# Two-layer adapted residual, fp32: tiles 0 and 1 multiplied in plain fp32, loads and selections reordered, last tile in two pieces

## What is computed

```python
x = x + einsum('bct,bcd->bdt', x, L0_weights[i0])      # (32,64,512), a 64x64 matrix for each sample
H = einsum('btd,od->bto', x, W)                        # 512x512, the same for all samples
xa = einsum('btd,brd->btr', x, A[i1])                  # rank 16, one of 8 adapters for each sample
x = x + H + einsum('btr,bor->bto', xa, Bm[i1]) * s[i1]
```

## Time and profile before

| | |
|---|---|
| median of 3 runs | 85.75 us (85.62 to 85.75) |
| profiled execution | 86.49 us |
| its span, first to last instruction | 84.5 us |
| TensorE, matmuls busy | 74.8 us, 89% |
| VectorE / ScalarE / GpSimd busy | 55.0 / 47.4 / 37.7 us |
| DMA | 14.58 MB, mean 173 GB/s |

### The profile page before, as it was taken

The page is one execution under the profiler, slowest core; times in us unless marked ns, Lnnn a source line. Parts: engine busy times, 40 slices in busy tenths (PEclk is TensorE's granted clock), DMA queues, the critical chain, the costliest instruction groups (busy, mean ns, idle before and its releaser), DMA issues.

```text
span 84.5 us, 1975 instructions
## 1 busy us (share of the span) xinstructions
PE 74.8 (89%) x498; PEld 70.0 (83%) x498; DVE 55.0 (65%) x132; ACT 47.4 (56%) x101; POOL 37.7 (45%) x83
## 2 busy tenths in 40 slices
PE   2985769938999999999999999999999999999650
PEld 2972569927999999999999999999999999999530
DVE  3898923696987567756865686568656865666230
ACT  0656200918777575757575757575767666463610
POOL 3075599974171656265526553645364541000000
PEclk9999999999999999999999999999999999999995
DMA  1896747999937848987796779868705550303033
GB/s 12 328 388 165 142 137 159 216 206 197 211 81 143 307 160 284 265 255 136 206 237 220 122 214 232 224 130 249 231 37 136 144 215 10 124 4 124 0 124 128
DMA packets 12797, 14.58 MB, mean 173 GB/s; under 512 B 6898, under 2 KB 7154, under 8 KB 12786
## 3 DMA queue, kind: packets, MB, share of 16 engines
q1 hardware_dynamic: 7458, 9.31, 37.5%
q0 software_dynamic: 4608, 4.22, 23.1%
q10 hardware_dynamic: 720, 0.92, 3.5%
HBM read 10.23 MB, written 4.19 MB: 171 GB/s over the span
## 4 chain that ended last, share of the span: by engine, by line
PE 76%; DVE 8%; DMA 6%; ACT 2%; ACTq 2%; issue 1%; POOL 1%; POOLq 0%; DVEq 0%
PE z_ps L489 54%; DMA scale_sb<-scales 6%; PE out_ps L523 5%; PE out_ps L527 4%; PE out_ps L530 4%; PE out_ps L524 4%; PE v_ps L514 4%; DVE moving L380 1%; DVE w_low L389 1%; POOL moving L221 1%; ACTq L262 1%; DVE a_scaled L437 1%; ACT b_high L291 1%; DVE b_stack L407 1%; DVE a_table L441 1%
## 5 line engine op out<-in xcount | busy, mean ns | idle before, releaser
L489 PE MATMUL z_ps<-moving,x_high 128*128 128x272 f32 x256 | 40.8, 299 | 2.6 <-POOL moving L221 1.4
L489 PEld LDWEIGHTS z_ps<-moving,x_high 128*128 128x128 f32 x256 | 36.7, 195 | 5.2 <-ACT moving L274 2.1
L398 DVE TENSOR_TENSOR z_low<-z_ps,z_high 128x240 fp32r<-128x240 f32 (+1 forms) x32 | 13.6, 424 | 17.3 <-ACT z_high L284 17.3
L228 POOL DMA_DIRECT2D b_raw<-b_t x32 | 19.7, 619 | 6.3 <-issue 6.2
L489 PE MATMUL z_ps<-moving,x_low 128*128 128x272 f32 x128 | 22.1, 297 | 0.0
L284 ACT ACTIVATE z_high<-z_ps 128x240 fp32r<-128x240 f32 (+1 forms) x32 | 12.3, 384 | 16.3 <-DVE low_rank L418 8.3
L489 PEld LDWEIGHTS z_ps<-moving,x_low 128*128 128x128 f32 x128 | 19.0, 197 | 0.0
L221 POOL CAST moving<-a_table 128x128 fp32r x32 | 9.0, 311 | 21.5 <-PE z_ps L489 20.6
L310 ACT ACTIVATE out_sb<-out_ps 128x512 f32<-128x512 f32 x15 | 9.0, 597 | 7.3 <-PE out_ps L530 7.3
L407 DVE TENSOR_TENSOR b_stack<-b_raw,b_high 128x512 fp32r<-128x512 f32 x16 | 11.1, 692 | 2.6 <-ACT b_high L291 2.6
L291 ACT ACTIVATE b_high<-b_raw,low_rows 128x512 fp32r<-128x512 f32 x16 | 11.4, 716 | 0.0
(11 more groups left out here) (33 smaller groups left out, 48.9 us busy)
## 6 DMA issues: line engine op xcount, KB each, us to landing
x_raw<-xt SPq DMA_DIRECT2D x16, 256.0 KB, 5.1
b_raw<-b_t POOLq DMA_DIRECT2D x32, 128.0 KB, 4.8
out<-out_sb SPq DMA_DIRECT2D x15, 256.0 KB, 4.0
w_raw<-w_t ACTq DMA_DIRECT2D x2, 256.0 KB, 3.2
w_raw<-w_t SPq DMA_DIRECT2D x2, 256.0 KB, 4.5
w_sb<-w SPq DMA_DIRECT2D x32, 16.0 KB, 3.7
a_raw<-a_t ACTq DMA_DIRECT2D x1, 256.0 KB, 5.1
out<-out_sb ACTq DMA_DIRECT2D x1, 128.0 KB, 1.7
```

The costliest lines, as they stand in the source:

```text
L228: pool.dma_start(b_raw[s * C:(s + 1) * C, t % BBUFS, :], b_t[ds(which[s], 1), :, :].to_broadcast([GROUPS, RANK, OUT]),).then_inc(b_loaded[ ...
L398: nc.vector.tensor_tensor(out=z_low[:, t % 2, col:col + n], in0=z, in1=z_high[:, t % 2, col:col + n].bitcast(fp32), op=ALU.subtract).then_ ...
L489: last = nc.tensor.matmul(z_ps[t % 2][:, bank, BANK_AT[bank]:BANK_AT[bank] + HALF], x[:, t % XBUFS, k * P:(k + 1) * P], moving[:, int(n == ...
```

## The change

- W is loaded in four pieces instead of four row blocks: first columns 0 to 271, then the rest, each in two halves of the rows (`PIECES`). x1 and A go ahead of the second column half, x2 ahead of w0. The scales move from ScalarE's queue to GpSimd's.
- The diagonal is added on VectorE in five parts (`DIAGONAL`), not on GpSimd.
- Tiles 0 and 1 (`PLAIN`) are multiplied in plain fp32 straight from `x_raw` and `w_raw`, four products for each bank instead of twelve. Their A columns are copied, scaled, into `w_raw` by ScalarE, which reads the indices itself. z is copied out whole (`z_plain`), and layer 0 is one fp32 matmul plus the low rank.
- TensorE's order: W bank of 0, A bank of 1, A bank of 0, W bank of 1; the low ranks and layer 0 of both lie among tile 2's banks.
- In the later tiles ScalarE and VectorE split B behind the low rank's v instead of ahead of z.
- The last tile's layer 0 is made in two pieces, A part and W part, in two PSUM tensors, with the layer 0 of tile 14 ahead of them and behind the last product.
- Eight warm-ups on a `warm` tile set by VectorE, not nine on the identity.

The diff, cut to its core:

```diff
+    PIECES = [(cols, rows) for cols in ((0, HALF), (HALF, OUT)) for rows in ((0, K // 2), (K // 2, K))]
+
+    DIAGONAL = ((0, 0, P, 0), (1, P, 2 * P, 0), (2, 2 * P, HALF, 1), (2, HALF, 3 * P, 3), (3, 3 * P, 4 * P, 3))
+
+    ADDED = (2, 3, 0, 5)
...
             load_x(0)
-            load_w(2)
+            load_w(1)
+            load_x(1)
             load_w(3)
+            load_x(2)
             sync.wait_ge(index_loaded, 16)
-            which = read_indices(sync, 0, 0, w0.shape[0], READ)
+            which = read_indices(sync, 0, 0, w0.shape[0], 2 * READ)
             sync.wait_ge(w0_cleared, 1)
             load_w0(which[0], 0)
-            load_x(1)
             load_w0(which[1], 1)
-            load_x(2)
-            which = read_indices(sync, 0, 2, w0.shape[0], READ)
-            load_w0(which[0], 2)
-            load_w0(which[1], 3)
             load_x(3)
+            load_w0(which[2], 2)
+            load_w0(which[3], 3)
             for t in range(4, TILES):
...
+            pool.dma_start(scale_sb[:], scales.rearrange("(a n) -> a n", a=1).to_broadcast([P, ADAPTERS]),
+                           ).then_inc(scales_loaded, 16)
             pool.wait_ge(ident_ready, 1)
             pool.wait_ge(index_loaded, 16)
-            which = read_indices(pool, 1, 0, ADAPTERS, READ)
-            for k in range(K):
-                add_diagonal(k)
+            which = read_indices(pool, 1, 0, ADAPTERS, 2 * READ)
+            pool.wait_ge(w_loaded[3], 16)
             load_b(which[0], 0)
             pool.wait_ge(a_ready, 1)
-            take_a(which[0], 0)
+            take_a(which[2], 2)
             load_b(which[1], 1)
             add_identity(0)
-            take_a(which[1], 1)
             add_identity(1)
-            for t in range(2, TILES):
+            load_b(which[2], 2)
+            take_a(which[3], 3)
+            add_identity(BATCH_OF[3])
+            load_b(which[3], 3)
+            for t in range(4, TILES):
...
             load_w(0)
-            load_w(1)
             act.dma_start(a_raw[:], a_t).then_inc(a_loaded, 16)
-            act.dma_start(scale_sb[:], scales.rearrange("(a n) -> a n", a=1).to_broadcast([P, ADAPTERS]),
-                          ).then_inc(scales_loaded, 16)
+            load_w(2)
             act.wait_ge(warm_ready, 1)
-            nc.scalar.activation(warm[0:1, 1:2], warm[0:1, 0:1], ACT.Copy)
-
-            def high_of_w(k):
-                act.wait_ge(w_diag, k + 1)
-                nc.scalar.activation(moving[:, 0, k, AC:AC + OUT], w_raw[:, k, :], ACT.Copy).then_inc(w_high_ready, 1)
+            nc.scalar.activation(warmed[:], warm[0:1, 0:1], ACT.Copy)
+            act.wait_ge(index_loaded, 16)
+            first = read_indices(act, 1, 0, ADAPTERS, PLAIN)
...
+            def take_raw_a(t):
+
+                at = 0 if t % 2 else AC + OUT
+                for s in range(PER):
+                    dst = w_raw[:, :, at + s * RANK:at + (s + 1) * RANK]
+                    src = a_raw[:, ds(first[t][s], 1), :].rearrange("p a (k r) -> p (a k) r", k=K)
+                    nc.scalar.activation(dst, src, ACT.Copy,
+                                         scale=scale_sb[:, ds(first[t][s], 1)]).then_inc(raw_cols_ready, 1)
...
+            def take_z(t, part):
+
+                z, col, n = z_part(t, part)
+                if part == A_PART:
+                    act.wait_ge(plain_rank_ready[t], 1)
+                else:
+                    act.wait_ge(w_bank_done, t + 1)
+                nc.scalar.activation(z_plain[:, t, col:col + n], z, ACT.Copy).then_inc(z_plain_ready[t], 1)
...
             high_of_w(0)
+            act.wait_ge(a_loaded, 16)
+            act.wait_ge(scales_loaded, 16)
+            take_raw_a(1)
+            take_raw_a(0)
             high_of_w(1)
+            take_z(0, W_PART)
+            act.wait_ge(a_scaled_ready, 1)
+            nc.scalar.activation(a_table[:, :, 0, :], a_scaled[:], ACT.Copy).then_inc(a_high_ready, 1)
             high_of_w(2)
             high_of_w(3)
-            act.wait_ge(a_scaled_ready, 1)
-            nc.scalar.activation(a_table[:, :, 0, :], a_scaled[:], ACT.Copy).then_inc(a_high_ready, 1)
+            take_z(1, A_PART)
+            high_of_x(2)
+            take_z(0, A_PART)
+            take_z(1, W_PART)
             act.wait_ge(low_rows_ready, 1 + PER)
-            high_of_z(0, A_PART)
             high_of_b(0)
-            high_of_z(0, W_PART)
             act.wait_ge(low_groups_ready, 1)
-            high_of_x(2)
             high_of_v(0)
-            high_of_z(1, A_PART)
             high_of_b(1)
+            high_of_v(1)
             high_of_x(3)
-            high_of_v(1)
+            high_of_z(2, A_PART)
+            high_of_x(4)
+            high_of_v(2)
+            high_of_b(2)
+            take_out(0)
+            take_out(1)
             last = TILES - 1
-            for t in range(2, TILES):
+            for t in range(3, last):
                 high_of_z(t - 1, W_PART)
-                high_of_b(t)
                 if t + 2 < TILES:
                     high_of_x(t + 2)
                 high_of_z(t, A_PART)
                 high_of_v(t)
-                if t == 2:
-                    take_out(0)
+                high_of_b(t)
                 take_out(t - 1)
+            high_of_z(last - 1, W_PART)
+            high_of_b(last)
+            high_of_z(last, A_PART)
+            high_of_v(last)
             high_of_z(last, W_PART)
+            take_out(last - 1)
+            _, col, n = z_part(last, A_PART)
             act.wait_ge(out_done, last + 1)
-            nc.scalar.activation(out_sb[:, last, 0:OUT // 2], out_ps[last % 2][:, 0:OUT // 2],
+            nc.scalar.activation(out_sb[:, last, col:col + n], out_ps[last % 2][:, 0:n],
                                  ACT.Copy).then_inc(out_ready, 1)
             act.wait_ge(out_ready, TILES)
-            act.dma_start(out[PER * last:, :, 0:OUT // 2].rearrange("s c l -> (s c) l"),
-                          out_sb[:, last, 0:OUT // 2]).then_inc(stored, 16)
+            act.dma_start(out[PER * last:, :, col:col + n].rearrange("s c l -> (s c) l"),
+                          out_sb[:, last, col:col + n]).then_inc(stored, 16)
             act.wait_ge(stored, 16 * (TILES + 1))
...
+            add_diagonal(0)
+            add_diagonal(1)
+            add_diagonal(2)
             dve.wait_ge(a_loaded, 16)
             dve.wait_ge(scales_loaded, 16)
             every = scale_sb[:].rearrange("p (a q) -> p a q", q=1).to_broadcast([P, ADAPTERS, K * RANK])
             nc.vector.tensor_tensor(out=a_scaled[:], in0=a_raw[:], in1=every, op=ALU.mult).then_inc(a_scaled_ready, 1)
-            low_of_w(2)
-            low_of_w(3)
+            low_of_w(0)
+            low_of_w(1)
+            add_diagonal(3)
+            add_diagonal(4)
             dve.wait_ge(a_high_ready, 1)
             nc.vector.tensor_tensor(out=a_table[:, :, 1, :], in0=a_scaled[:],
                                     in1=a_table[:, :, 0, :].bitcast(fp32),
                                     op=ALU.subtract).then_inc(a_ready, 1)
-            high_of_x(1)
-            low_of_x(1)
-            split_w0(0)
             dve.wait_ge(own_rank_ready, 1 + PER)
+            take_low_rank(1)
+            low_of_w(2)
+            low_of_w(3)
             take_low_rank(0)
-            low_of_z(0, A_PART)
+            low_of_x(2)
+            take_low_rank(2)
             low_of_b(0)
-            low_of_z(0, W_PART)
-            split_w0(1)
-            low_of_x(2)
             low_of_v(0)
-            take_low_rank(1)
-            low_of_z(1, A_PART)
             low_of_b(1)
+            low_of_v(1)
             low_of_x(3)
-            low_of_v(1)
+            low_of_z(2, A_PART)
+            low_of_x(4)
+            low_of_v(2)
+            low_of_b(2)
+            split_w0(BATCH_OF[2])
             last = TILES - 1
-            for t in range(2, TILES):
+            for t in range(3, last):
                 low_of_z(t - 1, W_PART)
-                low_of_b(t)
                 take_low_rank(t)
                 low_of_z(t, A_PART)
                 if t + 2 < TILES:
                     low_of_x(t + 2)
                 low_of_v(t)
+                low_of_b(t)
                 if t % 2 == 0:
                     split_w0(BATCH_OF[t])
+            low_of_z(last - 1, W_PART)
+            take_low_rank(last)
+            low_of_z(last, A_PART)
+            low_of_b(last)
+            low_of_v(last)
             low_of_z(last, W_PART)
-            dve.wait_ge(out_ready, TILES)
-            nc.vector.tensor_copy(out_sb[:, last, OUT // 2:], out_ps[last % 2][:, OUT // 2:]).then_inc(last_ready, 1)
+            _, col, n = z_part(last, W_PART)
+            dve.wait_ge(last_done, 1)
+            nc.vector.tensor_copy(out_sb[:, last, col:col + n], v_ps[(last + 1) % 2][:, 0:n]).then_inc(last_ready, 1)
...
+            def plain_products(t, part, ks):
+
+                at = FIRST[t % 2] + bank_of(t, part) * HALF
+                for k in ks:
```

(61 more changed lines are left out.)

162 lines of the change are left out of this document (92 added, 70 removed).

## The result

The changed kernel takes **83.02 us** (median of four executions) against 85.75 before: ratio 0.966, 95% interval 0.958 to 0.973. Now and then an execution of either kernel falls in a slower state (here one at 85.77, beside three at 82.84 to 83.03), and the ratios in this document leave such executions out. It is faster, by less than half of the 6.6 us forecast, and its time lies above the range of 77.8 to 82.3. Its profiled execution took 83.01 us.

The account below looks back on a forecast made before the run. It took TensorE (4.16 us a tile) to bound the even stretch and a relay of waits the beginning. Start 13.9 − 21.3, moved work +1.8, crossing +0.3, end −1.3 sum to −6.6: 85.75 to 79.1 us, range 77.8 to 82.3.

Parts of the forecast that it names:

- Price of a plain product: Tiles 0 and 1 on TensorE: a plain fp32 product of 272 columns takes 0.47 us fast, 0.945 slow.
- change of pace: Start: TensorE goes from slow to fast pace at 7.5 us, so tile 2 starts at 13.9.
- the pace changes late: Rival, start: TensorE's pace changes only at 11 us, losing 1.7 us, 80.8 us in all; chance 0.16.
- Do the data keep up?: Start: loads at 402 GB/s plus 0 to 1 us land before TensorE wants them, slack 1.2 or more each.
- The scales on GpSimd's queue: Start: the scales land at 3.9, 6.4 or 8.8 us, taken 6.4; ScalarE wants them at 5.6 to 7.
- helpers late: Rival: A copies or scales arrive 1.5 us late, or the crossing costs 1.5; 80.6 to 82.1 us, chance 0.16.
- The crossing: Behind tile 2's start, ScalarE and VectorE catch up on three tiles' work: +0.3 us, bounds 0 and 1.5.
- B behind the low rank costs nothing: Later tiles: splitting B behind the low rank costs nothing, as b_t is read only a tile later.
- The end: From last product to end: 4.5 us, 0.93 paid earlier before, against 4.9; −1.3 us, bounds −0.8 and −1.4.
- The period of 4.16: Even stretch of later tiles: TensorE's 4.16 us a tile stays unchanged.
- Slower: Rival: slow pace through all plain products, 85.5 us, or 86.7 with a slow first bank of tile 2; chance 0.04.
- no gain: Rival: a plain product costs twice the scaled pair, adding 6.6 us, 85.7 in all; chance 0.02.

Follow-up runs that it names:

- b0: The changed kernel itself run once more, with no edit, as a yardstick; ratio 0.957 to the kernel before.
- b2: Changed kernel without the scales' load (scale_sb set to 1) and with B of tile 1 loaded ahead of A's selection for tile 2; ratio 0.933.
- c3: Changed kernel with the scales' load doubled, the second into a buffer nothing reads; 83.89 us, one execution.
- e1: Kernel d1 with w0 of tiles 2 and 3 loaded ahead of x3 on SyncE's queue; ratio 0.925 to the kernel before.
- a3: Changed kernel with GpSimd's load of B for tile 1 moved ahead of A's selection for tile 2; ratio 0.940.
- c4: Changed kernel with B split ahead of the low rank again in tiles 3 to 14, as before the change; ratio 0.975.
- b3: Kernel before with the last-tile part of the change alone; ratio 0.987.
- d2: Kernel before with the scales loaded as one 32-byte row and spread by a matmul with ones; ratio 1.007.
- a1: Changed kernel with the scales' load back on ScalarE's queue, between W piece 0 and A; ratio 0.944.
- b1: Changed kernel with the edits of a1 and a3 together; ratio 0.949.
- d1: Changed kernel with scales as one row spread by matmul, and B of tiles 0, 1, 2 loaded in a row once W piece 1 landed; ratio 0.938.
- a4: Changed kernel with the load of x2 issued after w0 of tile 0; 83.08 us, one execution.

## Why the prediction was wrong

Predicted −6.65, measured −2.73: 3.9 us. Of this 0.5 is scale: the spans differ by 3.2, but the sum was made on an execution that was 0.74 above its median, and what lies around the span shrank by 0.28. The rest by the steps:

- **Price of a plain product and change of pace: held.** 0.45 against 0.47, and in after the pace changed at 7.3 against the 7.5 taken. Without its stand tile 2 would have started at 15.02 − 1.46 = 13.56, against 13.9. The 24 instructions behind 9.64 all run at the fast pace, and no slow pace past 8.5 was seen in after, so the rival *the pace changes late* falls. That 7.3 is so near 7.5 is luck: it was a choice without a row, and in b0, the same kernel, the pace had changed by 5.7.
- **"Do the data keep up?": the step that failed first, 1.3 us** (15.02 against 13.9; 0.16 of it from taking before's start from the chain and not the timeline). The sum gave x1 7.1 and piece 3 7.8, with 0 to 1 us on top; they came at 9.3 and 10.0, and the prediction's own sign of being wrong, a gap of TensorE between 5 and 14 us, is there. It counted bytes over 402 GB/s, and the scales are 4 KB. The runs put a price on these 4 KB in 128 pieces: 0.9 to 1.6 us on x1's landing for each such load (b2, after, c3). Before had the load too, but as the last one of ScalarE's queue, behind its two W blocks and A (and by time of issue behind all of W and x0).
- **"The scales on GpSimd's queue": 6.4 was taken, 8.7 came**, the late end of its bounds, the 8.8 of the earlier trace rows. With it the copies of A ran from 8.91 on. These are 0.33 each, as taken (0.3). So this rival, *helpers late*, is what happened, and on both sides. Its late end, 82.1, has 1.5 on each side; the start kept inside that (1.3 late), the crossing's stall did not (2.2). The forecast 79.1 with 1.3, 1.9 (the stall above the 0.3 of the sum), 0.2 of the end and 0.5 of scale comes to the 83.0 measured.
- **The crossing: the step that failed most, 1.9 us** (2.2 against 0.3, bounds 0 and 1.5). It added up VectorE's operations and found them done in time. They would have been: in e1, with loads in time, the stall is 0.7, and in a3 0.4. What it left out is *when GpSimd issues the B loads*. It noted "A copies, two B loads, end near 13" and asked when the identity was ready, not when the second B had landed. It was issued at 13.80 and took till 19.99, within the 2.3 to 7.2 of the earlier trace rows. Asking of each operation of the crossing "when does its input land" would have shown the stall from rows at hand: at the late end 13 + 7.2 = 20.2 for B, its two splits 1.4, `v_stack` 0.3, TensorE at 21.9; it was 21.69, and TensorE had been ready at 20.5. With the middle figure, 4.8, it is 19.5 and no stall: the rows gave a bound here, not a forecast.
- **"B behind the low rank costs nothing": wrong by its wait**, in the change's favour (c4: 2.52 against 0.39 before tile 3's low rank; in time 0.8 to 1.6, which the intervals don't secure). "b_t is read only a tile later" was about who reads it; what counts is what is queued behind it on VectorE.
- **The end: held**, −1.1 (b3 and after) against −1.3.
- **The period of 4.16: held** (four chain rows of 24 products in after start at 27.02, 31.17, 35.34 and 39.50).
- **Slower and no gain:** neither rival appears; a plain product takes 0.45, not twice the scaled pair.

The forecast start of 13.9 and nearly the small stall are both reached by e1 (12.73 and 0.7, against 0.3), so TensorE's part of the sum was right, and the supply of data that it took for granted was not there. That e1 starts 1.2 earlier than forecast is mostly the pace: it was fast from the first product, and by the prediction's own rate (a us later costs half a us) a change at 5.2 in place of 7.5 is worth 1.15.

## What to carry to other kernels

Sum a beginning by *landings*, not by bytes: for each operation of the first tiles write down who issues its input, what that queue does before, and issue plus the late end of the measured landing times. A load with many tiny rows counts by its rows: put it where little is under way, or load one row and spread it on chip (and see that the row delays nothing itself, as it did A in d2). When several loads in turn are the last, test whether each is late by its place before concluding that the memory is full: here one line moved in GpSimd's order (a3) was worth 1.8 us of the span, and one in SyncE's (e1) 1.5.

## What the runs showed of the hardware

- A load of 128 rows of 32 bytes takes the DMA engines from 327 to 144 GB/s for a microsecond at a busy share of 0.92 (after; 143 to 233 in the others with it once on GpSimd's queue), and takes 5.1 us (ScalarE's queue: before, a1, b1) to 7.1 us (GpSimd's) to land itself. On ScalarE's queue the slow microseconds of a1 and b1 have a busy share of only 0.27 to 0.41, on GpSimd's one of 0.88 or more; why is open. The Trainium skill ("DMA: Bandwidth & Descriptors", "Specifications") gives 512 bytes as the smallest transfer at full rate; the direction agrees with b2, after and c3, but it states no price that such a load has for the others.
- The granted clock can fall in the middle of a kernel. In c3 TensorE stood 2.40 us before 10.26. The windows then read
```profile
11.00:12.00 1.00, 1.00 (x4) 0.76 (x4) 1.00 (x4) 1.00 (x3) 0.38 (x1) 0.70 0.82 242
12.00:13.00 1.00, 1.00 (x4) 0.69 (x3) 0.40 (x1) 0.49 (x1) 1.00 (x3) 0.50 0.22 54
...
15.00:16.00 1.00, 1.00 (x6) 0.81 (x5) 0.08 (x1) 0.00 (x0) 1.00 (x3) 1.00 0.67 122
```
  with 0.50, the 1.2 GHz level, in the clock's column from 12 on, and the 24 instructions behind the stand took 7.46 us where they took 5.74 in after. In c4 the same followed a stand of 2.52. Those are two executions, each seen once, so how regular it is stays open. The stands of 1.46 in after, 1.90 in d1, 1.97 in a4 and 2.11 in c4 (before 9.91) brought no fall. So the stall in c3 cost 1.7 us more than itself.
